# When a latent layer's context matrices are computed: six groups in the layer before, two ahead of the own scores

## The reference

```
x = x + linear_attention(norm(x))             # layer 0: 16 heads, causal
x = x + cross_attention(norm(x), ctx)         # 16 heads
x = x + experts(norm(x))                      # 16 experts, top 2, capacity 640
x = x + latent_attention(norm(x))             # layer 1: 8 heads of 64, latent of 64
x = x + context_attention(norm(x), ctx)       # layer 1: ONE head of 256
x = x + quantised_feed_forward(norm(x))       # 768 wide

context_attention:  q = Q @ Wq + bq;  k = ctx @ Wk + bk;  v = ctx @ Wv + bv
                    P = softmax(mask(q @ k.T / 4));  out = (P @ v) @ Wo + bo
```

## Time and profile before

| what | us |
|---|---|
| median of 3 runs (lowest, highest) | 1782.88 (1778.44, 1787.87) |
| the profiled execution | 1775.84 |
| its span, first to last instruction | 1774.1 |
| busy: PE, DVE, ACT, POOL | 1552.3, 957.2, 827.6, 459.4 |
| mean granted TensorE clock | 0.942 |

### The profile page before, as it was taken

One profiled execution on the slowest core, in us unless ns is written; L12 is line 12 of the kernel. 1 busy time (PEld: TensorE's weight loads), 2 busy tenths in 40 slices (PEclk: granted clock), 3 DMA queues, 4 the chain that ended last, 5 costly groups with the idle time before them and its releaser, 6 DMA issues. The chain is left out here.

```text
span 1774.1 us, 26885 instructions
## 1 busy us (share of the span) xinstructions
PE 1552.3 (87%) x10059; PEld 1077.1 (61%) x10059; DVE 957.2 (54%) x2226; ACT 827.6 (47%) x1820; POOL 459.4 (26%) x582
## 2 busy tenths in 40 slices
PE   6999999998887399999996999999999879993099
PEld 3666766666665177787873666666666634441088
DVE  3565667756765343222214565566655445599932
ACT  4445564564464122212113556656656423596740
POOL 3222233343434300000006554454333200131000
PEclk9999999999998699999997999999999979997599
DMA  3430101011211144435343101110000000000211
GB/s 109 148 146 17 44 28 52 24 38 53 87 50 51 65 157 122 146 107 158 94 134 93 43 25 40 41 53 30 10 17 16 13 12 1 0 1 6 89 36 60
DMA packets 99680, 107.12 MB, mean 60 GB/s; under 512 B 25314, under 2 KB 88556, under 8 KB 99552
## 3 DMA queue, kind: packets, MB, share of 16 engines
q1 hardware_dynamic: 93408, 88.83, 16.1%
q0 software_dynamic: 6144, 16.57, 2.9%
HBM read 63.59 MB, written 42.01 MB: 60 GB/s over the span
## 5 line engine op out<-in xcount | busy, mean ns | idle before, releaser
L1876 ACT ACTIVATE c_pr<-bank,c_nmax 128x256 f32<-128x256 f32 x256 | 117.9, 474 | 151.1 <-DVE c_nmax L1957 132.0
L1629 POOL TENSOR_SCALAR c_pr<-c_pr,c_rsum 128x256 f32<-128x256 f32 x256 | 127.8, 514 | 224.0 <-DVE c_rsum L1962 223.8
L1396 ACT ACTIVATE b_G<-bank 128x320 f32<-128x320 f32 x128 | 56.0, 437 | 209.7 <-PE bank L1346 209.7
L1346 PE MATMUL bank<-b_XT,shared 128*128 128x320 f32 x512 | 153.5, 434 | 0.0
L1360 PE MATMUL bank<-shared,b_G 128*128 128x256 f32 x640 | 142.2, 379 | 0.0
L1360 PEld LDWEIGHTS bank<-shared,b_G 128*128 128x128 f32 x640 | 120.9, 190 | 17.8
L954 DVE TENSOR_TENSOR a_A<-bank,a_causal 128x512 f32<-128x512 f32 x128 | 79.4, 683 | 71.0 <-PE bank L480 70.9
L1957 DVE TENSOR_REDUCE c_nmax<-bank 128x2 f32<-128x512 f32 x128 | 82.2, 683 | 55.0 <-PE bank L1668 54.2
L415 POOL TENSOR_TENSOR a_L<-a_L,a_Lm 128x1232 f32<-128x1232 f32 x32 | 71.9, 2248 | 147.4 <-DVE a_Lm L969 147.4
L1346 PEld LDWEIGHTS bank<-b_XT,shared 128*128 128x128 f32 x512 | 91.8, 191 | 27.1 <-issue 0.4
L1415 DVE COPY b_Y<-bank 128x256 f32<-128x256 f32 x80 | 33.9, 424 | 120.3 <-PE bank L1360 120.1
(11 more groups left out here) (315 smaller groups left out, 3434.3 us busy)
## 6 DMA issues: line engine op xcount, KB each, us to landing
shared<-L_ffn_w SPq DMA_DIRECT2D x32, 512.0 KB, 6.2
t_slots_in<-a_h SPq DMA_DIRECT2D x20, 512.0 KB, 6.9
shared<-t_slots_in SPq DMA_DIRECT2D x15, 640.0 KB, 7.1
t_slots_out<-b_Y SPq DMA_DIRECT2D x15, 640.0 KB, 4.1
a_xin<-x SPq DMA_DIRECT2D x8, 512.0 KB, 3.8
a_xr<-x SPq DMA_DIRECT2D x8, 512.0 KB, 3.9
t_x_a<-hT_all SPq DMA_DIRECT2D x8, 512.0 KB, 2.9
shared<-t_x_a SPq DMA_DIRECT2D x8, 512.0 KB
```

Of the source, the lines that this page charges most:

```text
L1346: t = p.matmul(P[2 + n % 2][:, 0:HC], w1[e % 3][:, u, 128 * f:128 * f + 128], XT[e % 2][:, u, HC * m:HC * m + HC], start=(u == 0), stop=(u ...
L1629: p.tensor_scalar(pr[k][:, e, u, :], pr[k][:, e, u, :], rsum[k][:, e, u:u + 1], 1.0, ALU.mult, ALU.mult).then_inc(q.pr_ready, 1)
L1876: a.activation(pr[t % 2][:, e, u, :], P[e][:, S * u:S * u + S], ACT.Exp, bias=nmax[t % 2][:, e, u:u + 1], accum_out=sums[t % 2][:, e, u:u ...
```

## The change

- In layer0, NEARLY = 6 groups' context matrices are made in 24 units of TensorE (xk, xv, xm, vo of groups 0 to 5), placed at the end of steps 79 to 94 by the table LATER. Their banks are 0 to 3 in turn, which the scores have left. ScalarE copies xk, xv and xm, VectorE vo, at the end of the same step in its own list: the last lines of the body of each engine's loop over t.
- Their inputs (weights, biases, six groups' contexts) come by 23 DMAs, issued at step 65 ahead of the first experts' weights, into rooms of the experts' buffers that are free by then. The loads of slots wait for the units that read there.
- The results stay in hT_all, the columns that are the feed-forward's input later: group i's xm and its bias row in row 0, its vo in row 1. For this the buffers of layer0 that lay in hT_all and are still used (x1, x2, h1, hT1) get rooms of their own, and others that are free by step 79 (A, state, pk, xin, h0, hT0) go there.
- In layer1, groups 6 and 7 are made on TensorE between the absorbed weights and the first scores; ScalarE and VectorE copy them ahead of their loops. The context units are taken out of the steps and out of UNITS; scores, penalties and values read hT_all.
- In layer0 ScalarE takes `exponents` of steps 4 and 6 ahead of the copy of the logits and of the router's exponential, and VectorE the moments of step 3 ahead of two divisions.
- In feed_forward the gate's peak is turned behind unit 1 (was 3) and spread behind unit 2 (was 4); ScalarE makes a one-column sigmoid ahead of the first copies, and then gate_int(0), keep_up(2), sigmoid(0), gate_int(1), keep_up(3).

```diff
+NEARLY = 6
+def context_columns(p, bank, w, xT):         # 4 matmuls of 154 columns
+def context_scores(p, bank, wT, bias, kT):   # 6 matmuls of 154 columns
+def context_outputs(p, bank, w, vT):         # 4 matmuls of 256 columns
...
+        LATER = {79: "xk0", 80: "xv0 xk1", 82: "xv1", 83: "xm0", 84: "vo0", 85: "xm1 vo1", 86: "xk2 xv2", 87: "xk3",
+                 91: "xv3", 92: "xm2", 93: "vo2", 94: "xm3 vo3 xk4 xv4 xk5 xv5 xm4 vo4 xm5 vo5"}
+        later_units = [n for t in sorted(LATER) for n in LATER[t].split()]
+        def later_bank(name, j):
+            return P[later_units.index(f"{name}{j}") % 4]
...
                     if k == 1 and g == NG:
                         wait_full(s, "val3", NG - 1)
+                        for n, w in ctx_w.items():
+                            s.dma_start(w, io["L1_xattn_" + n]...).then_inc(q.l_in, 16)
+                        s.dma_start(ctx_bo, io["L1_xattn_bo"]...).then_inc(q.l_in, 16)
+                        for n in ("bq", "bk", "bv"):
+                            for u in range(2):
+                                s.dma_start(c.second[n][:, u:u + 1], ...).then_inc(q.l_in, 16)
+                        for j in range(NEARLY):
+                            for u in range(2):
+                                s.dma_start(ctx_x[j][:, u, :, :], ctx_cols[j, u]).then_inc(q.l_in, 16)
                         for e in range(3):
                             load_expert(s, c, io, e)
...
                 s.wait_ge(scattered, 16 * TOPK * NT * NG)
+                wait_later_made(s, "xv", 4)
                 load_first_slots(s, c, dr)
+                s.wait_ge(q.l_made, 4 * NEARLY)
...
+                def context_unit(name, j):
+                    n = later_units.index(f"{name}{j}")
+                    if n == 0:
+                        p.wait_ge(q.l_in, 16 * (11 + 2 * NEARLY))
+                        p.wait_ge(q.front_kept, 4 * front["x", NG - 1, NT - 1] + 4)
+                    if n >= 4:
+                        wait_later_kept(p, later_units[n - 4][:2], int(later_units[n - 4][2:]))
...
+                    for name, j in later_at(t):
+                        context_unit(name, j)
...
             @block.vector
...
+                    for name, j in later_at(t):
+                        if name == "vo":
+                            wait_later_made(v, name, j)
+                            v.tensor_tensor(later.vo[j], later_bank(name, j)[0:S2, :]..., bcast(ctx_bo[0:S2, :], 1, NB), ALU.add)
...
-                 1: (("turn0a", 1, 1), ("turn0b", 1, 1), ("xk", -1, 2), ("xv", -1, 2)),
+                 1: (("turn0a", 1, 1), ("turn0b", 1, 1)),
-                 3: (("lat", 1, 1), ("xm", -1, 2)),
+                 3: (("lat", 1, 1),),
-                 5: (("vo", -1, 1), ("q1", 1, 1), ("turn1a", -1, 1), ("turn1b", -1, 1)),
+                 5: (("q1", 1, 1), ("turn1a", -1, 1), ("turn1b", -1, 1)),
...
                 p.wait_ge(q.absorb_kept, 8)
+                p.wait_ge(sq.c_ctx_in, 32 * (NG - NEARLY))
+                for k in range(NG - NEARLY):
+                    context_columns(p, P[2 * k], xwk, ctxT[k]).then_inc(q.l_made, 1)
+                    context_columns(p, P[2 * k + 1], xwv, ctxT[k]).then_inc(q.l_made, 1)
+                for k in range(NG - NEARLY):
+                    p.wait_ge(q.l_kept, 2 * k + 2)
+                    context_scores(p, P[2 * k], xwqT, bq, kbT[k]).then_inc(q.l_made, 1)
+                    context_outputs(p, P[2 * k + 1], xwo, vbT[k]).then_inc(q.l_made, 1)
...
-                for u in range(2):
-                    v.tensor_copy(bqw[:, u, :], bq[:, u:u + 1].broadcast_to([128, 128])).then_inc(q.c_dve, 1)
+                for k in range(NG - NEARLY):
+                    v.wait_ge(q.l_made, 2 * (NG - NEARLY) + 2 * k + 2)
+                    v.tensor_tensor(vo[NEARLY + k], P[2 * k + 1][0:S2, :]..., bcast(bo[0:S2, :], 1, NB), ALU.add)
...
                     a.activation(raw[:, m % FC, T * (m // FC):T * (m // FC) + T], P[m % 8][:, :], ACT.Copy).then_inc(q.unit_kept, 1)
+                a.activation(gi[2][:, 0:1], inv["x"][:, :], ACT.Sigmoid)
-                for m in range(4):
+                for m in range(2):
                     keep_up(m)
                 a.wait_ge(q.scaled, 2)
                 gate_int(0)
+                keep_up(2)
+                sigmoid(0)
                 gate_int(1)
-                sigmoid(0)
+                keep_up(3)
```

More of the change, by code:

```diff
@@ L130, in fill_selector, with keep_context @@
     return n
+NEARLY = 6
+def context_columns(p, bank, w, xT):
+    KX = NB * S2
+    for m in range(2):
+        for u in range(2):
+            x = p.matmul(bank[:, KX * m:KX * m + KX], w[:, u, 128 * m:128 * m + 128],
+                         xT[:, u, :, :].rearrange("p b k -> p (b k)"), start=(u == 0), stop=(u == 1))
+    return x
+def context_scores(p, bank, wT, bias, kT):
+    KX = NB * S2
+    for m in range(3):
+        for u in range(2):
+            x = p.matmul(bank[:, KX * m:KX * m + KX], wT[:, u, 128 * m:128 * m + 128] if m < 2 else bias[:, u:u + 1].broadcast_to([128, 128]),
+                         kT[:, u, :, :].rearrange("p b k -> p (b k)"), start=(u == 0), stop=(u == 1))
+    return x
+def context_outputs(p, bank, w, vT):
+    for b in range(NB):
+        for u in range(2):
+            x = p.matmul(bank[0:S2, D * b:D * b + D], vT[:, u, b, :], w[:, u, :], start=(u == 0), stop=(u == 1))
+    return x
+def keep_context(a, out, bank, bias):
+    KX = NB * S2
+    for m in range(2):
+        x = a.activation(out[:, m, :, :].rearrange("p b k -> p (b k)"), bank[:, KX * m:KX * m + KX], ACT.Identity, bias=bias[:, m:m + 1])
+    return x
 def layer0(nc, ctx, c, io, dr):
@@ L158, in layer0 @@
         minus = sb("minus", [128, NT])
-        xin = sb("xin", [128, NT, D])
         xr = sb("xr", [128, NT, D])
-        late = [c.hT_all[:, n // 4, 1024 * (n % 4):1024 * (n % 4) + 1024].rearrange("p (j d) -> p j d", j=NT) for n in range(8)]
-        x1 = [late[k] for k in range(3)]
-        x2 = late[3]
+        early = [c.hT_all[:, n // 4, 1024 * (n % 4):1024 * (n % 4) + 1024] for n in range(8)]
+        x1 = [sb(f"x1_{k}", [128, NT, D]) for k in range(3)]
+        x2 = sb("x2", [128, NT, D])
         stats = [sb(f"stats_{n}", [128, NT, 6]) for n in range(3)]
@@ L921, in _ @@
                             keep_norm(0, g + 2, hT0)
+                        if back2:
+                            exponents(g - 2, 2)
                         if back4:
@@ L1180, in share @@
     pre["bo"] = c.expert_x[:, 2816:3072]
[L1181 removed]
+    pre["ctxT"] = [c.expert_x[:, at:at + 2 * NB * S2].rearrange("p (u b k) -> p u b k", u=2, b=NB) for at in (3072, 3536)]
     pre["imask"] = part(3380, (NB, S2), I32)
@@ L1187, in share @@
     c.second = pre
+    KX = NB * S2
+    rows = [c.hT_all[:, 0, T * i:T * i + 3 * KX] for i in range(NG)]
+    c.later = namedtuple("Later", "scores_row xm row vo")(
+        rows, [r[:, 0:2 * KX].rearrange("p (c b k) -> p c b k", c=2, b=NB) for r in rows],
+        [r[:, 2 * KX:3 * KX].rearrange("p (b k) -> p b k", b=NB) for r in rows],
+        [c.hT_all[0:S2, 1, T * i:T * i + T].rearrange("p (b n) -> p b n", b=NB) for i in range(NG)])
     c.second_signals = signals(nc, ctx, "c_w slot0_in slot1_in x0_in x1_in c_ctx_in")
@@ L1817, in _ @@
                         latent_keys(g + 1)
-                    if s == 5 and behind:
-                        x_outputs(g - 1)
                     if s == 5 and ahead:
@@ L1828, in _ @@
                         x_values(g - 2, 1)
-                    if s == 1 and behind:
-                        context("xk", g - 1, xwk)
-                        context("xv", g - 1, xwv)
-                    if s == 3 and behind:
-                        x_keys(g - 1)
                     if s == 4 and ahead:
@@ L1862, in keep_norm @@
                         keep_unit(f"turn{n}{half}", i, out[u], bank(f"turn{n}{half}", i)[:, :])
-                def keep_context(name, i, out, bias):
-                    wait_full(a, name, i)
-                    for m in range(2):
-                        a.activation(out[:, m, :, :].rearrange("p b k -> p (b k)"), bank(name, i)[:, KX * m:KX * m + KX], ACT.Identity,
-                                     bias=bias[:, m:m + 1]).then_inc(freed(name, i), 1)
                 def exponents(t):
```

169 lines of the change are left out of this document (87 added, 82 removed).

## The result

The changed kernel takes 1764.3 us (median of 4 runs, 1763.7 to 1764.9), the kernel before 1782.9 (4 runs, 1778.4 to 1787.9): ratio 0.990, 95% interval 0.988 to 0.991, or 18.6 us less. The forecast was 1757.7, so the gain is 6.6 us smaller than forecast. The two profiled executions lie closer together, 1775.8 and 1763.7 (spans 1774.1 and 1762.0), because the one before is 7 us quicker than its median. So by steps the forecast of -25.2 stands against -12.1, and the sum has to be looked at by stages.

A forecast was written before the change was run, and what follows sets the result against it. TensorE bounds the latent loop and idles in two stretches. +14.6 (VectorE's order) + 0 (units) - 2 (order) + 10 (prologue) - 43.8 (loop, drain) - 4 (feed-forward) = -25.2 us: 1750.6 from the profiled execution, 1757.7 by medians; range 1738 to 1776.

The forecast's parts named there:

- VectorE behind vo5, +14.6: Layer0's end: weigh(7) waits on VectorE for the last of ten units and its addition, delaying the experts 14.6 us.
- the rival of the low clock: Both empty stretches stay at the lower clock, costing 30 and 20 us: no change, 1783 us; chance 0.12.
- the rival of hidden tails: The empty stretches do hide the work, so the 14.6 us shrink to near 0: 1743 us; chance 0.17.
- The fourteen other units and the order, 0 and -2: Layer0, steps 79 to 93: units cost 0 (bounds -2, +8.3); exchanged order gives -2 us (bounds -4, +3).
- The prologue, +10: Latent layer before its loop: mix(0) waits on VectorE for two additions of vo; 10 us cost, bounds 8 and 20.
- Loop, -39.8: Latent layer's loop: context work leaves TensorE, 6.0 us less per steady group, 39.8 us less in all.
- Steps 3 and 4: Latent loop: ScalarE takes over the pace, so both steps together give 1.9 us a group, not 3.8.
- The drain, -4: Behind the latent loop: output matrix and columns no longer delay the last group's turn and projection; 4.0 us less.
- Feed-forward, -4: Gate's peak turned earlier and table load ahead of the copies: activate(0) starts earlier, 4 us less, bounds 1 and 5.
- A group of 7.9 us less: Latent loop: all 7.9 us a group come back, 10 us more gain, 1748 us; chance 0.12.
- "Paced by VectorE and ScalarE": Latent loop: TensorE only fills the pace, so removing its work gives only the drain's 4; +14.6, 1797 us; chance 0.06.

The follow-up runs named there:

- the kernel with `weigh` moved first: Changed kernel with VectorE's additions of vo3, vo4 and vo5 of step 94 moved behind weigh(7): 1738.8 us, ratio 0.980 to the kernel before.
- 7.6 us came back with the order: Changed kernel with VectorE's two prologue additions of vo moved behind the first norm, so mix(0) goes ahead: 1739.8 us, ratio 0.981 to the kernel before.
- The dummies ahead of the turn and behind it: Changed kernel plus dummy matmuls: two ahead of step 3's turn, 1764.8 us (0.996 of the kernel before); or four behind it, before step 4's scores, 1758.5 (0.991).
- 1.8 us in step 2: Changed kernel with four dummy matmuls more in project(g - 1, 1), step 2 of each group: 1764.5 us, ratio 0.996 to the kernel before.
- the one attempt: Kernel before with only xm and lat exchanged in step 3's unit order, giving the latent transposes another bank: 1778.8 us, ratio 1.004.

## Why the prediction was right, and where its terms were off

The direction, the mechanism and the time within the range held; what came out 13 us short of the sum by the profiled pair (6.6 by the medians) is spread over four terms. The kernels of the experiments leave most stages as they are, so their traces give each stage more than once. With medians over them, the shortfall moves to one place: from the first scores to the turn of the peak, loop and drain together, it takes 473.9 us in four traces without the change and 437.1 in five with it. That is 36.7 us less, where 43.8 were forecast. This is the term that was mis-sized.


- **VectorE behind vo5, +14.6: right.** It was 13.5, and undoing that one order gave 12.9 back. The experts start at 640.75; 639 was named. The clock was 0.97 there, as assumed, so the rival of the low clock fell at this place, and the rival of hidden tails fell for this kernel. What that rival describes is the kernel with `weigh` moved first.
- **The fourteen other units and the order, 0 and -2: within their bounds.** The last ranks came 2.7 us later in the first pair. Over all traces, the eight with units and exchanges reach them at 596.8 to 606.2 (median 598.3), the four with neither at 597.2 to 603.5 (median 597.8), which settles nothing. A shorter distance tells more, from the ranks of step 78 to the last ones, since all fourteen units stand between them: 49.4 to 50.1 us with them (median 49.4), 45.6 to 48.9 with neither (median 46.9), 45.9 with the exchanges alone. So the units cost 0.5 to 4.5 us, by the medians 2.6, where 0 was taken. The clock did give back, as forecast: it was 0.97 there in all eight and 0.68 to 0.78 without the units. It gave back most of the 8.3 us that they take, not all. What the exchanges brought stays open.
- **The prologue, +10: 13.1 in the first pair, 9.7 by the medians.** The step was right (7.6 us came back with the order). Where the low clock falls differs between executions: five traces of kernels without the change have 33.2 to 35.5 us (median 35.1), five with it and its order have 41.4 to 46.3 (median 44.9). The columns ran partly at the low clock (6.13 to 7.33 us), so mix(0) came 8.1 to 11.1 us late for the 8.7 worked out at the full clock. The queries ran at the low clock in most traces of both sorts, but not in the first trace of the kernel before. The 10 was a fair lean, and the first pair an unlucky one.
- **Loop, -39.8: -36.7.** Steady group 5.4 for 6.0: steps 1 and 5 gave 2.10 and 1.68 for 2.2 and 1.9, steps 3 and 4 gave 1.66 for 1.9. The first group gave 4.35 for 5.8 (step 1 gave 2.8 and step 2 took 1.5 back), and the last 2.2 for 4. Five of seven groups were steady ones, and two of these also lost a dip of the clock of 1.6 us each that the trace of before has in step 4 (58.85 us). Without these 3.2 us the loop had given 33.5; the second pair of traces gives 34.2.
- **Steps 3 and 4, the reason:** the prediction split them as ScalarE's pace, with 0.3 us of copy gone and q0 next, and that sum was about right. The dummies ahead of the turn and behind it show what the mechanism is: from the turn of step 3 on VectorE and ScalarE run back to back until q0, so the score matrix, which stood behind that turn, gave nothing by itself. The rows agree: the 1.8 us by which q0 comes nearer lie behind the exponents of step 4, where the wait for the penalties and the 0.3 us copy of the score matrix stood. That wait alone was not removed in any run, as the one attempt passed it on, so its price by itself is argued.
- **The drain, -4: -0.6.** The mechanism was right (the turn 3.8 us earlier), the term failed: with TensorE emptier the clock is low from 1402 on, and the 3.2 us by which the rest took longer ate it. That holds in every trace: from that turn to the turn of the peak it is 26.5 us in the eight with the change and 23.1 to 23.3 in the five without. The prediction had looked at the clock in both empty stretches, but not in the stretch from which it took work away.
- **Feed-forward, -4: -4.4** up to the down product (5.0 for the whole stage), and the edits alone gave the same 4.4.
- **Rivals.** A group of 7.9 us less did not come (5.4). "Paced by VectorE and ScalarE" fell as a whole, since 1.8 us in step 2 cost 1.7; but it holds for step 4, where the same 1.8 us cost nothing.

## What to carry to other kernels

Work moved into an engine's empty stretch is paid by whoever reads its result in order: look at every engine's list for what stands behind the copy out of the bank. Here additions of vo placed behind the chain's next instructions take back all that the two stretches had cost (13.5 us, and 9.7 by the medians), and turn a gain of 1.1% into one of 2.7%. To find what sets a step, put known work back at two places in it: what it costs ahead of and behind a hand-over tells where the chain begins, which the busy shares and the single wait named in the trace don't.

## What was not expected of the hardware

Taking work out of a full stretch cost clock: in the drain the granted clock was 0.67 after the change and 0.78 before (1380.8 to 1429.6, and 1387.3 to 1436.7). Putting work into an emptier one gave clock back: at layer0's end 0.97 with the fourteen units, 0.68 to 0.78 without. And the layer0 part of the same kernel took 606.2 and 602.8 us in two executions of the changed kernel, 603.5 and 597.2 in two of the kernel before, with the low clock at different places each time (from 400 to 500 us, ahead of every unit, it was 0.93 and 0.90 in the one, 0.95 and 1.00 in the other). So a single pair of profiled spans can be off by 6 us for a reason that has nothing to do with the change.
